# Q's spread begun by ScalarE, the gate by a power on GpSimd, centred output weights, new orders on every engine

## The reference

```
x = x + conv3x3(relu(gn(x) * mask(gn(x))))        # mask from each image's centre of mass
x = x + ttt(layernorm(gn(x) as 784 tokens of 128))
```

```
xq, xk, xv = rope(x Wq), rope(x Wk), x Wv         # 16 x 16 each
Z1   = xk W1 + b1
grad = gradient of a layer norm of Z1 against xv - xk
eta  = token weight * sigmoid(x . lr_w + lr_b) / 16      # the gate
out  = xq + layernorm(xq W1 - (eta*tril(xq xk^T)) grad + b1 - tril(eta) grad)
W1, b1 = W1 - (last_eta*xk)^T grad, b1 - sum(last_eta*grad)
y    = layernorm(out, over 128) * post_w + post_b, times Wo
```

## Time and profile before

| | us |
|---|---|
| median of 3 runs | 2010.93 |
| lowest, highest | 2007.13, 2014.58 |
| span of the profiled execution, first to last instruction | 2010.2 |

### The profile page before, as it was taken

How to read it: one execution, slowest core, us unless ns; L and a number is a source line. 1 busy time by engine, 2 the same in 40 slices (tenths; PEclk the granted TensorE clock), 3 DMA queues, 4 the chain that set the end, 5 groups by cost and what they waited for, 6 DMA issues and landing times.

```text
span 2010.2 us, 82699 instructions
## 1 busy us (share of the span) xinstructions
PE 1569.5 (78%) x33518; PEld 1214.9 (60%) x33518; DVE 1582.3 (79%) x3818; ACT 977.5 (49%) x2358; POOL 1317.2 (66%) x1479
## 2 busy tenths in 40 slices
PE   1886978914678887888788888878887888888886
PEld 1443544502567676677676766766776766767664
DVE  6989998706687877788878878887888788788774
ACT  2223545443455555555555545555555555555452
POOL 1244535465677777777767777777777777677763
PEclk9998989965666667666656666666666666666655
DMA  6058697962555655556656556666565566566553
GB/s 235 1 30 44 98 98 68 77 159 45 65 70 66 76 71 68 73 67 77 74 65 77 70 69 74 72 71 73 67 77 73 67 77 73 65 76 73 69 68 44
DMA packets 1656796, 148.89 MB, mean 74 GB/s; under 512 B 1636448, under 2 KB 1650016, under 8 KB 1656416
## 3 DMA queue, kind: packets, MB, share of 16 engines
q1 hardware_dynamic: 1396912, 117.90, 49.9%
q10 hardware_dynamic: 259504, 25.70, 10.1%
HBM read 40.71 MB, written 38.54 MB: 39 GB/s over the span
## 4 chain that ended last, share of the span: by engine, by line
SPq 54%; PE 17%; DVE 12%; DMA 7%; issue 6%; POOL 3%; ACT 2%; POOLq 0%; DVEq 0%; ACTq 0%
SPq L486 25%; SPq L519 13%; SPq L479 12%; DMA late<-work 3%; PE p_m L1678 3%; PE p_x L1693 3%; DMA xs_scratch<-work 2%; SPq L438 2%; PE p_j L1557 2%; DVE work L1007 2%; SPq L440 1%; DVE work L1033 1%; PE p_y L1736 1%; PE p_y L1693 1%; PE p_out L1752 1%
## 5 line engine op out<-in xcount | busy, mean ns | idle before, releaser
L1648 PE MATMUL p_kt<-fold,kqk 128*128 128x16 f16 x6272 | 199.4, 174 | 166.9 <-DMA kqk<-work 162.8
L1648 PEld LDWEIGHTS p_kt<-fold,kqk 128*128 128x128 f16 x6272 | 190.6, 104 | 197.9 <-issue 161.3
L808 ACT ACTIVATE work<-p_kt 128x512 f16<-128x512 f32 x196 | 146.9, 750 | 317.8 <-PE p_kt L1648 317.8
L1557 PE MATMUL p_j<-work 128*128 128x392 f16 x864 | 158.5, 345 | 22.2 <-DVE work L1131 20.7
L578 POOL TENSOR_TENSOR work<-work,row 128x256 f32<-128x256 f32 x98 | 96.9, 988 | 113.2 <-DVE work L1437 113.2
L1316 DVE TENSOR_TENSOR work<-work 128x256 f16<-128x256 f32 x196 | 155.2, 842 | 15.4 <-ACT work L795 15.4
L1621 PE MATMUL p_j<-wa,work 128*128 128x512 f16 x196 | 119.4, 609 | 58.4 <-DMA work<-xs_scratch_tail 30.0
L590 POOL TENSOR_TENSOR w<-wst,w 128x256 f16<-128x256 f32 x98 | 75.5, 770 | 127.8 <-ACT w L855 127.8
L1693 PEld LDWEIGHTS p_x<-w,late 128*128 128x128 f16 x4704 | 149.5, 106 | 12.0
L634 POOL TENSOR_TENSOR work<-work,rope_s 128x256 f32<-128x256 f32 x196 | 141.0, 740 | 20.0 <-DVE work L1283 20.0
L645 POOL TENSOR_TENSOR work<-work 128x512 f32<-128x512 f32 x98 | 130.8, 1335 | 30.4 <-DVE work L1307 30.1
(11 more groups left out here) (171 smaller groups left out, 4474.3 us busy)
## 6 DMA issues: line engine op xcount, KB each, us to landing
late<-work SPq DMA_DIRECT2D x1176, 32.0 KB, 2.7
kqk<-work SPq DMA_DIRECT2D x392, 64.0 KB, 4.2
out_y<-work ACTq DMA_DIRECT2D x49, 256.0 KB, 6.4
x_scratch<-late SPq DMA_DIRECT2D x24, 392.0 KB, 11.7
xs_scratch<-work SPq DMA_DIRECT2D x24, 392.0 KB, 6.7
work<-x_scratch ACTq DMA_DIRECT2D x49, 192.0 KB, 3.4
work<-xs_scratch SPq DMA_DIRECT2D x48, 192.0 KB, 3.4
late<-in_x SPq DMA_DIRECT2D x8, 784.0 KB, 9.0
```

Of the source, the lines that this page charges most:

```text
L808: return act.activation(kqt16[:, o, g:g + GP, :, :, :].rearrange("p g h t a -> p g a (h t)"), p_kt[:, :].rearrange("p (g a n) -> p g a n", ...
L1557: mm = pe.matmul(p_conv[b % 2][h][:, 0:HALF].rearrange("o (i j) -> o i j", j=W), convw16[:, w, t, :], pad[:, b % 2, a, r:r + ROWS, c:c + W ...
L1648: mm = pe.matmul(p_kt[:, at:at + CS], part_of(g + k, h, a), fold16[:, :], start=True, stop=True)
```

## The change

- SyncE no longer begins Q's turned spread. ScalarE does, in `qt_spread`, with the same eight DMAs, semaphores and waits. Its place in ScalarE's turn is behind `qt_copy(2k-3)`, for chunk k-2.
- The gate is 1 / (1 + e^-l): GpSimd raises the constant 1/e to the power l (`rate_power`), VectorE adds one (`rate_denominator`) and takes the reciprocal (`rate_gate`). The Sigmoid on ScalarE is gone.
- The output weights are centred once: the mean over channels of `wo_p` is taken off it, by one product with a matrix of 1/128 and one subtraction. A constant added to a row then has no effect on the output, so `post_shift` is gone and `post_norm` only scales.
- Every engine's turn has a new order, and some steps stand in another turn. ScalarE's loop runs NCH + 6 turns instead of NCH + 5, SyncE's NCH + 3 instead of NCH + 4.

```diff
             def turn(k):
-                m_spread(k - 4)
                 kt_spread(k - 3)
-                qt_spread(k - 3)
+                xs_next(k)
                 kq_spread(k - 2)
-                xs_next(k)
-
-            for k in range(NCH + 4):
+                m_spread(k - 3)
+
+            for k in range(NCH + 3):
                 turn(k)
...
+            @guard_chunk
+            def rate_power(c):
+                pool.wait_ge(rate_scaled_done.sem, rate_scaled_done.count(c))
+                l = lgt[:, c % 3, :, :, :].rearrange("p a g h -> p (a g h)")
+                pool.tensor_tensor(l, inv_e[:, 0:1].to_broadcast([128, NG * NH]), l, ALU.pow).then_inc(rate_power_done.sem, 1)
+
...
             def turn(k):
+                k_scaled(2 * k - 1)
+                w_low(2 * k - 6)
+                target(2 * k - 1)
+                q_out(2 * k - 1)
+                b_low(2 * k - 5)
                 rope_sin(2 * k)
+                w_low(2 * k - 5)
+                g_scaled(2 * k - 4)
+                g_hat(2 * k - 4)
+                g_dot(2 * k - 4)
+                rope_sum(2 * k)
                 o_scaled(2 * k - 6)
                 o_sum_q(2 * k - 6)
+                rate_power(k - 1)
+                k_scaled(2 * k)
                 g_both(2 * k - 4)
-                rope_sum(2 * k)
-                k_scaled(2 * k)
+                target(2 * k)
                 g_scaled(2 * k - 3)
-                target(2 * k)
+                q_out(2 * k)
                 g_hat(2 * k - 3)
                 g_dot(2 * k - 3)
-                q_out(2 * k)
                 rope_sin(2 * k + 1)
                 o_scaled(2 * k - 5)
+                o_sum_q(2 * k - 5)
                 g_both(2 * k - 3)
+                rope_sum(2 * k + 1)
                 b_low(2 * k - 4)
-                o_sum_q(2 * k - 5)
-                w_low(2 * k - 4)
-                rope_sum(2 * k + 1)
-                k_scaled(2 * k + 1)
-                q_out(2 * k + 1)
-                target(2 * k + 1)
-                b_low(2 * k - 3)
-                w_low(2 * k - 3)
-                g_scaled(2 * k - 2)
-                g_hat(2 * k - 2)
-                g_dot(2 * k - 2)
 
...
             @guard_chunk
+            def qt_spread(c):
+                act.wait_ge(qt_copy_done.sem, qt_copy_done.count(2 * c + 1))
+                if c < 2:
+                    act.wait_ge(s_kt_zero[c], 1)
+                else:
+                    act.wait_ge(o_done.sem, o_done.count(2 * c - 3))
+                part, whole = turned_parts(c, 0)
+                for b in range(GB):
+                    at = slice(b * CS, (b + 1) * CS)
+                    act.dma_start(whole[at, :, b, :], part[at]).then_inc(qt_landed.sem(c), 16)
+
...
             def post_norm(s):
-                act.wait_ge(post_shift_done.sem, post_shift_done.count(s))
+                act.wait_ge(post_inverse_done.sem, post_inverse_done.count(s))
                 if s >= 1:
                     act.wait_ge(post_turn_done.sem, post_turn_done.count(s - 1))
                 for k in range(GP):
-                    last = act.activation(on[:, k * C:(k + 1) * C], oo[:, k * C:(k + 1) * C], ACT.Identity, bias=ostd[:, 2, k:k + 1],
-                                          scale=ostd[:, 1, k:k + 1])
+                    last = act.activation(on[:, k * C:(k + 1) * C], oo[:, k * C:(k + 1) * C], ACT.Copy, scale=ostd[:, 1, k:k + 1])
                 last.then_inc(post_norm_done.sem, 1)
...
             def turn(k):
+                y_store(k - 6)
+                o_square(2 * k - 8)
+                post_root(2 * k - 9)
+                b_high(2 * k - 7)
+                o_root(2 * k - 8)
+                z_square(2 * k - 6)
+                post_norm(2 * k - 9)
+                z_root(2 * k - 6)
+                w_high(2 * k - 7)
+                xr_load(k - 4)
+                m_high(k - 3)
+                x_square(2 * k - 1)
+                qk_high(2 * k - 2)
+                o_square(2 * k - 7)
                 ln_root(2 * k - 1)
+                z_square(2 * k - 5)
+                kt_copy(2 * k - 4)
                 z_root(2 * k - 5)
+                post_copy(2 * k - 9)
                 post_root(2 * k - 8)
-                o_square(2 * k - 7)
-                post_copy(2 * k - 9)
-                g_high(2 * k - 6)
-                kt_copy(2 * k - 4)
                 o_root(2 * k - 7)
                 kt_copy(2 * k - 3)
+                g_high(2 * k - 6)
                 post_norm(2 * k - 8)
-                qk_high(2 * k - 2)
+                qt_copy(2 * k - 4)
+                post_copy(2 * k - 8)
                 b_high(2 * k - 6)
-                qt_copy(2 * k - 4)
-                y_store(k - 5)
+                qt_copy(2 * k - 3)
+                qt_spread(k - 2)
+                g_high(2 * k - 5)
+                qk_high(2 * k - 1)
                 w_high(2 * k - 6)
-                qt_copy(2 * k - 3)
-                g_high(2 * k - 5)
-                post_copy(2 * k - 8)
                 x_square(2 * k)
-                o_square(2 * k - 6)
-                qk_high(2 * k - 1)
-                post_root(2 * k - 7)
-                o_root(2 * k - 6)
-                b_high(2 * k - 5)
                 ln_root(2 * k)
-                z_square(2 * k - 4)
-                w_high(2 * k - 5)
-                z_root(2 * k - 4)
-                post_norm(2 * k - 7)
-                rate_gate(k - 1)
-                m_high(k - 2)
-                xr_load(k - 3)
-                x_square(2 * k + 1)
-                z_square(2 * k - 3)
-
-            for k in range(NCH + 5):
+
+            for k in range(NCH + 6):
...
+                folded(dve.tensor_tensor(wo_p[:, :], wo_p[:, :], p_x[1][:, SC:SC + C], ALU.subtract))
...
+            @guard_chunk
+            def rate_denominator(c):
+                dve.wait_ge(rate_power_done.sem, rate_power_done.count(c))
+                if c >= 3:
+                    dve.wait_ge(z_rate_done.sem, z_rate_done.count(2 * (c - 3) + 1))
+                dve.tensor_scalar(gate[:, c % 3, :, :, :].rearrange("p a g h -> p (a g h)"),
+                                  lgt[:, c % 3, :, :, :].rearrange("p a g h -> p (a g h)"), 1.0, None,
+                                  ALU.add).then_inc(rate_denominator_done.sem, 1)
+
+            @guard_chunk
+            def rate_gate(c):
+                dve.wait_ge(rate_denominator_done.sem, rate_denominator_done.count(c))
+                flat = gate[:, c % 3, :, :, :].rearrange("p a g h -> p (a g h)")
+                dve.reciprocal(flat, flat).then_inc(rate_gate_done.sem, 1)
...
             def turn(k):
+                m_low(k - 3)
+                g_means(2 * k - 6)
+                g_along(2 * k - 6)
+                g_centre(2 * k - 6)
+                qk_low(2 * k - 2)
+                post_stats(2 * k - 8)
+                z_sum(2 * k - 5)
+                post_aggr(2 * k - 8)
+                ln_inverse(2 * k - 1)
+                o_sum(2 * k - 7)
+                z_inverse(2 * k - 5)
+                g_rated(2 * k - 6)
+                z_hat(2 * k - 5)
+                post_inverse(2 * k - 8)
+                o_inverse(2 * k - 7)
+                b_step(2 * k - 6)
+                z_rate(2 * k - 5)
+                final(2 * k - 9)
                 norm(2 * k - 1)
-                o_inverse(2 * k - 7)
+                g_low(2 * k - 6)
+                rope_cos(2 * k - 1)
+                o_hat(2 * k - 7)
                 g_means(2 * k - 5)
-                final(2 * k - 9)
-                o_hat(2 * k - 7)
+                g_centre(2 * k - 5)
                 g_along(2 * k - 5)
-                g_centre(2 * k - 5)
                 w_step(2 * k - 6)
-                qk_low(2 * k - 2)
+                rate_scaled(k - 1)
+                rate_denominator(k - 2)
+                post_stats(2 * k - 7)
                 g_rated(2 * k - 5)
-                rope_cos(2 * k - 1)
+                rate_gate(k - 2)
+                post_aggr(2 * k - 7)
                 g_low(2 * k - 5)
-                post_stats(2 * k - 7)
-                rate_scaled(k - 1)
-                post_aggr(2 * k - 7)
+                qk_low(2 * k - 1)
+                ln_inverse(2 * k)
                 b_step(2 * k - 5)
+                norm(2 * k)
                 o_sum(2 * k - 6)
-                qk_low(2 * k - 1)
                 post_inverse(2 * k - 7)
                 w_step(2 * k - 5)
                 z_sum(2 * k - 4)
-                post_shift(2 * k - 7)
                 o_inverse(2 * k - 6)
+                o_hat(2 * k - 6)
                 z_inverse(2 * k - 4)
-                ln_inverse(2 * k)
                 z_hat(2 * k - 4)
+                m_mask(k - 2)
                 final(2 * k - 8)
-                norm(2 * k)
                 z_rate(2 * k - 4)
-                m_mask(k - 2)
-                o_hat(2 * k - 6)
-                g_means(2 * k - 4)
                 rope_cos(2 * k)
-                g_along(2 * k - 4)
```

(30 more changed lines are left out.)

56 lines of the change are left out of this document (18 added, 38 removed).

## The result

The changed kernel takes 2055.2 us (median of 4, 2052.5 to 2056.7) against 2012.8 of the kernel before, run beside it: a ratio of 1.022, 95% interval 1.018 to 1.025. It is slower, by about 2%. The forecast was 1913, the range 1810 to 1985: wrong in sign and outside the range. The profiled execution took 2056.7 us, its span is 2054.9.

The account below looks back on a forecast made before the run. SyncE's issuing of 34 transfers was taken as the bound at 30.69 us a period. The new loop, 13.8 + 5.6 + 9.25 = 28.65 us, saves 2.04 over 48 periods, 98 us: 1913 us, range 1810 to 1985.

Parts of the forecast that it names:

- SyncE bound the kernel, and loses its place as bound: SyncE: issuing 34 transfers fills some 30.5 of 30.69 us a period; with 26 it needs 23.3 to 25.1.
- The ring 13.8 + X + K: Loop through PE folds, ScalarE's Q issues, g_high, qk steps, SyncE's K/Q issues and landing: 28.65 us, ends 26.0 and 32.8.
- K: Time of SyncE's eight K/Q block issues (kq_spread): 6.8 us alone to 11.7 beside two large ScalarE transfers, taken as 9.25.
- X: Time of the eight issues of Q's spread on ScalarE: between 5.4 and 7.3 us, taken as 5.6.
- The power: GpSimd's 128x32 power per chunk: taken as 1 us, possibly 0.1 to 5, hidden up to about 2.7; GpSimd's load 23.9.
- VectorE's sum and reciprocal: Gate steps on VectorE, 128x32: 0.1 to 0.3 us each, 0.4 together, waiting for nothing.
- X + K: Sum of ScalarE's Q issues and SyncE's K/Q issues: above 16.9 us the rival "the loop at its long ends" decides.
- the loop at its long ends: Rival, chance 0.15 (0.07 for slower): both issue times at their longest, period 32.8 us, 2111 us.
- xr_load waits for y_store, 2 to 3 us, costed at nothing: ScalarE: the x load waits for the y store to land, 2 to 3 us idle; nothing added, ScalarE having room.
- Centring 0: Centred output weights: VectorE sheds 1.3 us a period, post_norm perhaps 0.4 on ScalarE; prologue work under 1 us, counted 0.
- Table loads worth nothing beyond their place: ScalarE: both 1283 ns table loads go with the Sigmoid; nothing credited beyond the place they free.
- The new orders move nothing between engines, so the sums hold: Reordered turns of all engines: nothing moves between engines beyond the stated changes; PE has 25.7 us of work.

Follow-up runs that it names:

- d1: Kernel before, old orders, with Q's spread on ScalarE in two parts of four issues where less urgent work follows: 1940.7 us, ratio 0.965.
- a4: Changed kernel with Q's spread given back to SyncE, power, centring and new orders kept: 2145.2 us, ratio 1.066.
- a1: Changed kernel with the power on GpSimd replaced by a product and 20 added in place of 1: 2029.8 us, ratio 1.007.
- a5: Changed kernel with the y store moved from the turn's start to its old place ahead of qt_copy(2k-3): 2185.7 us, ratio 1.087.
- b3: Kernel before with only the gate changed: power on GpSimd, sum and reciprocal on VectorE, no Sigmoid: 2128.1 us, ratio 1.057.
- a8: Changed kernel with y_store(k-6) moved ahead of kt_copy(2k-4) and xr_load(k-4) ahead of qt_copy(2k-3): 2122.5 us, ratio 1.055.
- b4: Kernel before with only the output weights centred and the shift gone: 2012.6 us, ratio 1.000.
- a3: Changed kernel with a product in place of the power and Q's spread behind g_high, qk_high and w_high: 2179.3 us, ratio 1.082.

## Why the prediction was wrong

- *SyncE bound the kernel, and loses its place as bound.* Right: gaps of 5.1 us a period, no wait of PE for K^T among its longer ones, and d1 and a4 show what the move is worth: 1940.7 against 2011 us in the old orders, with the issues in two parts, and 90 us in the new ones.
- *The ring 13.8 + X + K.* The right structure: each piece of the timeline releases the next, and grad and qk_low end within 0.06 us of each other, as laid out. The fixed part is 13.85 by the medians, put at 13.8. That it is so near is in part luck: the sum held no wait for the power, and without the power (a1) the fixed part is 31.22 - 11.54 - 6.23 = 13.45.
- *K.* The step that failed. The prediction gave 6.8 alone, 9.25 beside one large ScalarE transfer, 11.7 beside two, and chose 9.25, hoping that one would fall behind the last issue. The timeline has both inside: the y store starts 0.5 us before the first K/Q issue, since the same late steps (g_high, qk_high) stand ahead of both, and the x load 6 us on. K is 11.47, +2.2. It can be taken apart. Before the change, with the x load inside in most turns, it was 8.57 (the 9.25 was one turn of 36, so a large transfer costs 8.57 - 6.81 = 1.8 us, not 2.4). With the x load alone inside it is 9.53 in the new kernel (a5), so 1.9 us go with the y store and 1.0 with the class of traces that has `inv_e`, near the 1.1 of the first eight issues (6.81 to 7.87). The first is shown by one edit. The second sets old orders beside new ones; within the old orders it is 0.8 (b3, 9.32).
- *X.* 6.32 against 5.6, +0.7, inside the bounds of 5.4 to 7.3. With K's 2.2 this makes 28.65 + 2.9 = 31.6, the measured period.
- *The power.* 5.6 us against 1, outside the bounds of its price (0.1 to 5). The rule "hidden up to 2.7 us" would have made 2.9 us of that; a1 and the wait at g_rated show 0.4 to 0.5. The load of GpSimd, 28.2 us, was put at 23.9 and is the highest of any engine.
- *VectorE's sum and reciprocal*, 0.4 us together, take 0.8; VectorE isn't the bound.
- *X + K.* 11.5 + 6.3 = 17.8, over the 16.9 from which the rival "the loop at its long ends" decides. It got 0.15, of which 0.07 for slower. That was the case that came, 42 of the 100 us to its end of 2111. Its "against" (Q's transfers are small) overlooked that K and X need not be at their ends for it: 16.9 - 14.85 = 2.05 us above the forecast's sum are enough.
- *What nobody had priced.* The longer issues of the class with `inv_e`: part of K, X and landing (4.2 to 5.3 us), and most of b3's 117 us, since there SyncE is full and its issues grew as much as the period. In the changed kernel the 1.0 us of K alone would be 48 us, an estimate from a5 against before, and the whole loss is 44.7. So without it the change might have come out even; no run of the new orders lacks `inv_e`, and this stays open, like the cause of the class.
- *xr_load waits for y_store, 2 to 3 us, costed at nothing.* m_high (L837) stands 123.2 / 43 = 2.9 us a period behind ScalarE's queue, but that holds the two issues of the x load too. In the turn shown, ScalarE is idle from 1005.05, the x load begins at 1006.64 and m_high at 1008.49: 1.6 us of waiting and 1.8 of issues. Whether it costs time isn't shown, since a8, which moves it, loses more elsewhere.
- *Centring 0.* Right (b4). *Table loads worth nothing beyond their place.* No run takes them out alone.
- *The new orders move nothing between engines, so the sums hold.* Not shown to be the fault. Where both orders can be compared in one class, with Q's spread on SyncE (a4 and b3), the new ones cost 17 us. The parts give 101 us in the old orders and 20 in the new ones, but there the class and the power go with the orders.

## What to carry to other kernels

When a queue's issue time is the bound, moving issues to another engine pays only if what stands behind them there can wait: eight issues are a block of 6 us of that engine's program, so cut them into twos or threes and put each where the next step has slack. Sum the new ring with every large transfer that the new order starts beside it, not with one; two transfers that follow the same steps start together, turn after turn. And after adding a buffer, however small, compare the transfer engines' busy share at equal GB/s with the version before, in a stretch that the edit did not touch: here it fell apart into two classes, whatever the cause.

## What the runs showed of the hardware

- A power on GpSimd, 128x32 in f32, takes 5.60 us (5.42 in b3), 0.175 us for each element of a partition. A product of the same shape in its place takes 0.42 us in a1 and 0.24 in a3, products on 128x256 0.73 to 1.03 on average. VectorE's sum on 128x32 takes 0.45, its reciprocal 0.34.
- The transfers of the scan keep the transfer engines busy for 0.60 of the time in the traces without `inv_e` (before, b4) and for 0.70 in b3 with it, at 72 and 67 GB/s, and a K/Q issue then has a median of 826 or 1114 ns. A kernel's first eight K/Q issues take 6.7 to 7.2 us without `inv_e` and 7.8 to 8.3 with it, in 20 traces. That the address of the buffers does this is argued, not shown.
- A 256 KB store stretches the issues of the engine that began it as well as the other's: eight of ScalarE's went from 6.32 to 9.14 us when it was put ahead of them (a5), and SyncE's eight K/Q issues from 11.47 to 9.53 when it was taken from them.
